# DLRM tower on one Trainium2 core: first indices in one small load spread by matmuls, first comparisons as tensor_scalar, another load order, and copies at a chunk's end split over two engines

## The reference

```python
e = jnp.stack([tbl_0[ids[:, 0]], ..., tbl_25[ids[:, 25]]], axis=1)      # (2048, 26, 128)
sd = jnp.einsum('bfd,bd->bf', e, dense)
ss = jnp.einsum('bfd,bgd->bfg', e, e)
z = jnp.concatenate([dense, sd, ss[:, iu, ju]], axis=1)                 # pairs above the diagonal
h = jnp.concatenate([z, dense], axis=1)
h = jnp.maximum(h @ W_top1 + b_top1, 0.0)                               # 607 -> 512
h = jnp.maximum(h @ W_top2 + b_top2, 0.0)                               # 512 -> 256
y = h @ W_top3
```

## Time and profile before

| | |
|---|---|
| time, 3 runs | median 418.59 us (418.02 to 419.38) |
| profiled execution | 415.0 us, its span 413.2 us |
| busy: PE, DVE, ACT, POOL | 344.1, 240.2, 191.2, 263.4 us |
| read from HBM | 34.90 MB |

### The profile page before, as it was taken

The page is one execution under the profiler, slowest core; times in us unless marked ns, Lnnn a source line. Parts: engine busy times, 40 slices in busy tenths (PEclk is TensorE's granted clock), DMA queues, the critical chain, the costliest instruction groups (busy, mean ns, idle before and its releaser), DMA issues.

```text
span 413.2 us, 12249 instructions
## 1 busy us (share of the span) xinstructions
PE 344.1 (83%) x5416; PEld 258.2 (62%) x5416; DVE 240.2 (58%) x454; ACT 191.2 (46%) x283; POOL 263.4 (64%) x279
## 2 busy tenths in 40 slices
PE   0816888569999998769999997879999996865797
PEld 0504445358878886357878885468778883554673
DVE  3827999538899860048799850068899720111421
ACT  2341103587712325756722326768413318794333
POOL 6777750377777777777777773777777755773000
PEclk9977998999999999869999999889999999996999
DMA  7998230133333322333333311424333211221000
GB/s 167 274 277 245 79 83 25 40 97 86 110 88 99 83 58 57 78 88 88 106 102 86 86 51 32 97 75 108 90 96 97 70 46 38 60 56 35 4 2 0
DMA packets 21332, 35.72 MB, mean 86 GB/s; under 512 B 8023, under 2 KB 10583, under 8 KB 21279
## 3 DMA queue, kind: packets, MB, share of 16 engines
q0 software_dynamic: 8704, 17.84, 17.0%
q1 hardware_dynamic: 12574, 17.09, 15.4%
HBM read 34.90 MB, written 0.01 MB: 84 GB/s over the span
## 4 chain that ended last, share of the span: by engine, by line
PE 64%; DVE 10%; DMA 8%; ACT 7%; issue 5%; POOL 5%; SPq 0%; POOLq 0%; ACTq 0%; DVEq 0%
PE late_bank L406 10%; PE late_bank L473 10%; PE gram_bank L440 10%; PE late_bank L407 9%; DVE one_hot L730 7%; PE turn_bank L424 6%; DMA table_ids<-in_ids_by_table_dram 6%; POOL rows L385 5%; PE turn_bank L406 4%; PE turn_bank L407 4%; ACT turned L617 3%; PE spare_bank L507 2%; PE late_bank L518 2%; PE gram_bank L507 2%; DVE table_lo L798 2%
## 5 line engine op out<-in xcount | busy, mean ns | idle before, releaser
L385 POOL DMA_INDIRECT rows<-in_tbl_dram,index x272 | 262.5, 965 | 113.0 <-issue 79.0
L730 DVE TENSOR_TENSOR one_hot<-table_ids,row_number 125x512 fp32r<-125x512 int32 x288 | 178.2, 681 | 39.9 <-PE turn_bank L407 15.3
L406 PE MATMUL late_bank<-one_hot,table_hi 125*128 125x512 f32 x192 | 85.9, 447 | 26.0 <-DVE one_hot L730 14.6
L617 ACT COPY turned<-turn_bank 128x512 f32<-128x512 f32 (+1 forms) x80 | 76.6, 1051 | 28.5 <-PE turn_bank L424 25.9
L407 PE MATMUL late_bank<-one_hot,table_lo 125*128 125x512 f32 x192 | 78.2, 407 | 0.0
L424 PE MATMUL turn_bank<-ident,rows 128*128 128x128 f32 x288 | 46.9, 293 | 24.1 <-ACT turned L617 17.6
L440 PE MATMUL gram_bank<-turned 128*27 128x26 f32 x4096 | 55.1, 194 | 12.7 <-issue 11.7
L406 PEld LDWEIGHTS late_bank<-one_hot,table_hi 125*128 125x128 f32 x192 | 37.9, 197 | 43.8 <-DVE table_lo L798 15.5
L440 PEld LDWEIGHTS gram_bank<-turned 128*27 128x27 f32 x4096 | 45.7, 107 | 28.8 <-issue 25.0
L284 DVE COPY gram<-gram_bank 124x208 f32<-124x208 f32 x32 | 12.0, 374 | 88.1 <-PE gram_bank L440 84.0
L424 PEld LDWEIGHTS turn_bank<-ident,rows 128*128 128x128 f32 x288 | 34.7, 149 | 37.4 <-issue 28.7
(11 more groups left out here) (64 smaller groups left out, 288.8 us busy)
## 6 DMA issues: line engine op xcount, KB each, us to landing
table_ids<-in_ids_by_table_dram SPq DMA_DIRECT2D x36, 256.0 KB, 3.3
rows<-in_tbl_dram,index POOLq DMA_INDIRECT x272
turned<-in_tbl_dram SPq DMA_DIRECT2D x6, 448.0 KB, 12.2
looked_up<-in_tbl_dram SPq DMA_DIRECT2D x3, 448.0 KB, 7.6
rows<-in_r_dense_features_dram SPq DMA_DIRECT2D x16, 64.0 KB, 2.4
gram<-in_W_top_dram SPq DMA_DIRECT2D x1, 702.0 KB
gram<-in_W_top_dram SPq DMA_DIRECT2D x2, 256.0 KB
looked_up<-in_W_top_dram SPq DMA_DIRECT2D x1, 512.0 KB
```

What stands on the lines that cost most here:

```text
L385: pool.indirect_dma_start(out=rows[:, row % RING_ROWS, :], out_offset=None, in_=tables[f], in_offset=bass.IndirectOffsetOnAxis(ap=index[:, ...
L406: pe.matmul(bank, table_hi[:, s, k, :], hot, start=k == 0, stop=False)
L617: nc.scalar.copy(to[:, f0:f1], of).then_inc(rows_copied, 1)
L730: nc.vector.tensor_tensor(one_hot[:, n % HOT_SLOTS, :], table_ids[0:RK, (c * LOOKUPS + s) % ID_SLOTS, :], row_number[0:RK, k:k + 1].broadc ...
```

## The change

1. **Indices of chunk 0.** The 9 broadcast loads of 256 KB are replaced by one load of the 26 index rows (26x512, 52 KB) into a slot of `table_ids`. VectorE casts them to float32; a TensorE matmul a table with a column of the identity, broadcast, as its weights writes that table's indices to 125 partitions of PSUM (`spread_ids`); ScalarE copies them to one of two slots at the end of `looked_up` (`copy_ids`). Later chunks load their indices as before.
2. **Comparisons of chunk 0** read this float32 copy and become `tensor_scalar` with a row number per partition in SBUF as the scalar. Those of later chunks stay `tensor_tensor` with the row numbers in PSUM.
3. **Order.** The index array for the gathers comes in three pieces (tile 0, tiles 1 to 3, the rest behind the weights) in place of two. The raw weights move to `gram` and one slot of `looked_up`. ScalarE rounds the tables between its other copies instead of all first, and splits the weights before the last two `copy_found`. Two memsets of PSUM fall away.
4. **Copies at a chunk's end and at the start.** Of tile 0, VectorE now does `place_found` and the row groups 1 and 3, ScalarE the groups 0, 2 and 4. `rows_copied` becomes two semaphores by bank. For tiles 1 to 3 nothing moves.

```diff
-            sp.dma_start(index[:, 0:1, :], index_tiles[:, 0:1, :]).then_inc(index_loaded[0], DMA)
-            load_ids(0, 0)
+            load_index(0)
+            sp.dma_start(id_rows, ids_t[:, 0:CHUNK]).then_inc(id_rows_loaded, DMA)
             load_table(0)
             load_dense(0, 0)
-            sp.dma_start(index[:, 1:, :], index_tiles[:, 1:, :]).then_inc(index_loaded[1], DMA)
-            load_table(1)
-            load_ids(0, 1)
-            for s in range(2, LOOKUPS):
+            load_index(1)
+            for s in range(1, LOOKUPS):
                 load_table(s)
-            load_dense(0, 1)
-            load_ids(0, ID_SLOTS)
+                if s == 4:
+                    load_dense(0, 1)
             for to, of in weight_loads:
                 sp.dma_start(to, of).then_inc(weights_loaded, DMA)
+            load_index(2)
...
+            def spread_ids(s):
+                if s == 0:
+                    pe.wait_ge(ident_made, 2)
+                    pe.wait_ge(id_values_made, 1)
+                if s >= ID_BANKS:
+                    pe.wait_ge(ids_copied, s - ID_BANKS + 1)
+                f = LOOKED_UP[s]
+                pe.matmul(id_bank(s), ident[0:26, f:f + 1].broadcast_to([26, RK]), id_values,
+                          start=True, stop=True).then_inc(ids_spread, 1)
+            for s in range(ID_BANKS):
+                spread_ids(s)
             for s in range(LOOKUPS):
                 pe.wait_ge(lo_made, s + 1)
                 look_up(0, range(s * K_ROWS, (s + 1) * K_ROWS))
+                if s + ID_BANKS < LOOKUPS:
+                    spread_ids(s + ID_BANKS)
...
+            round_table(0)
+            copy_ids(0)
+            round_table(1)
+            copy_ids(1)
+            round_table(2)
+            round_table(3)
+            for s in range(2, LOOKUPS):
+                copy_ids(s)
+                if s - 2 == LOOKUPS - 3:
+                    act.wait_ge(w1_merged, 1)
+                copy_found(0, range((s - 2) * K_ROWS, (s - 1) * K_ROWS))
+                if s + 2 < LOOKUPS:
+                    round_table(s + 2)
...
-                    nc.vector.tensor_tensor(one_hot[:, n % HOT_SLOTS, :], table_ids[0:RK, (c * LOOKUPS + s) % ID_SLOTS, :],
-                                            row_number[0:RK, k:k + 1].broadcast_to([RK, CHUNK]), ALU.is_equal).then_inc(one_hot_made, 1)
+                    hot = one_hot[:, n % HOT_SLOTS, :]
+                    if c == 0:
+                        last = nc.vector.tensor_scalar(hot, id_slot(s), row_number_sb[:, k:k + 1], None, ALU.is_equal)
+                    else:
+                        last = nc.vector.tensor_tensor(hot, table_ids[0:RK, (c * LOOKUPS + s) % ID_SLOTS, :],
+                                                       row_number[0:RK, k:k + 1].broadcast_to([RK, CHUNK]), ALU.is_equal)
...
                 if more:
-                    copy_rows(c + 1, 0, range(0, 2))
-                    place_found(c + 1, 0)
+                    copy_rows(act, c + 1, 0, (0,))
                 for n in range(N2):
                     relu2(c, n)
                 if more:
-                    copy_rows(c + 1, 0, range(2, TURNS))
+                    copy_rows(act, c + 1, 0, (2, 4))
                 copy_output(c)
...
                     split_h1(c, n)
+                if more:
+                    place_found(dve, c + 1, 0)
+                    copy_rows(dve, c + 1, 0, (1, 3))
```

More of the change, by code:

```diff
@@ L185, in dlrm_tower @@
         pairs = turned[:, (TILES - 1) % 2].rearrange("p i f -> p (i f)")[:, 0:GROUP * PAIRS].rearrange("p (q f) -> p q f", q=GROUP)
+        raw = [room[0:RK, n * K_ROWS * D:(n + 1) * K_ROWS * D]
+               for room in (looked_up[:, 0:LOOKUPS - 2].rearrange("p s b -> p (s b)"), turned[:].rearrange("p a i f -> p (a i f)"))
+               for n in range(room.shape[1] // (K_ROWS * D))][0:LOOKUPS]
         late_room = gram[:].rearrange("p a f -> p (a f)")
@@ L217, in dlrm_tower @@
         w2_lo_made = sem("w2_lo_made")
[L218 removed]
+        index_loaded = [sem(f"index_loaded{i}") for i in range(len(FIRST_TILES))]
+        id_rows_loaded = sem("id_rows_loaded")
+        id_values_made = sem("id_values_made")
+        ids_spread = sem("ids_spread")
+        ids_copied = sem("ids_copied")
         dense_loaded = [sem(f"dense_loaded{i}") for i in range(RING_TILES)]
@@ L693, in _, with round_table @@
             act.sem_inc(stored, DMA)
-            for s in range(LOOKUPS):
+            def round_table(s):
                 act.wait_ge(table_loaded[s], DMA)
```

161 lines of the change are left out of this document (90 added, 71 removed).

## The result

The changed kernel takes 395.67 us (median of 4 runs, 395.58 to 396.11) beside 418.99 us before (4 runs, 418.02 to 420.06): a ratio of 0.9445, 95% interval 0.9419 to 0.9471. That is 23.3 us faster, or 19.3 us by the profiled executions (415.0 to 395.68; spans 413.2 to 393.9). The forecast was 404.4 with a range of 398 to 413: a gain of up to 20.6 us, which the 23.3 between the medians exceed and the 19.3 between the profiled executions would not. Medians leave out disturbed runs.

The account below looks back on a forecast made before the run. The prediction took TensorE as the main bound, with VectorE pacing the start and GpSimd's gathers the last chunk. Its terms, 19.0 - 5.0 - 5 + 5.2 = 14.2 us, off the 418.6 us median gave 404.4, range 398 to 413.

Parts of the forecast that it names:

- 19.0: Start: the most TensorE can be ahead at chunk 0's last gathers before GpSimd limits it, 19.0 us instead of 25.1.
- the holding: Start: VectorE work delays gathers, 5.0 us by `table_lo`, splits and `place_found`, and 5 us by the new comparisons.
- the ends: Chunk ends: splitting the copies lets group 4 be turned 2.6 us sooner at each of two ends, 5.2 us; the third counts nothing.
- the level: Total time: the 14.2 us gain is taken off the 418.6 us median, 3.6 above the profiled execution's 415.0.
- x = 5: Start: what the 72 new comparisons cost by stretching gathers, taken as 5 us.
- the one moment of a gather: Start: a comparison delays a gather only by catching one moment of it, for half its own length, 3.3 us in all.
- a hold for 65% of every comparison: Start: comparisons hold gathers for as large a part of their length as seven `table_lo` operations did, 16 us.
- the end hardly depends on it: Start: whether a comparison takes 0.34 us or stays at 0.60 was said to matter little to the final time.
- a rival at 403.3: Start: comparisons stay at 0.60 us and hold no gathers, gain 15.3 us, time 403.3; chance 0.13.
- first product at 59.5: End of the start: TensorE's first product comes at 59.5 instead of 84.65, up to 25.1 us ahead.
- GpSimd still waiting before tile 12: Last chunk: GpSimd still waits for tile 12's rows; if not, it bounds everything and the third-end argument changes.
- The rival "Slower": Start: each comparison waits for the gather in flight, one per 1.247 us, time about 445; chance 0.06.

Follow-up runs that it names:

- the doubled kernel: The changed kernel with each of chunk 0's comparisons made twice, once into an unused buffer: 423.18 us, ratio 1.0136 to the kernel before.
- `mix`: The changed kernel with the last four tables' comparisons of chunk 0 as `tensor_tensor`, the first five as changed: 396.41 us, ratio 0.9492 to the kernel before.

## Why the prediction was right or wrong

**The mechanism was right in the main.** The start was shortened until gathers bounded it, TensorE waits for them in the last tile of chunk 0 (at 87.95, 92.99 and 97.91, though not in the tile before it, as expected too), stretched gathers take some of it back, both kinds of term add up, and a comparison takes 0.40 us from start to start instead of 0.60. The Trainium skill, "VectorE: DVE Perf Modes", The perf-mode tier table, has the two forms at two elements and one a cycle. The trace (0.40 and 0.60 us) agrees with the direction; by halving the elements at an unchanged fixed part the forecast had 0.34, so the fixed part is larger here. Its sum was 19.0 - 5.0 - 5 + 5.2 = 14.2 us of span; measured were 13.6 to the end of chunk 0, 8.8 over the next two chunks and -3.2 behind tile 12, 19.3 unrounded.

**Three terms were mis-sized, all in the same direction:** the holding by 4.6 us (13.6 where 19.0 - 10 = 9.0 was forecast), the ends by 3.6, and the level by 4.0. The tail took 3.2 back, and the median of the kernel before came out 0.4 higher than the one that the forecast started from. That is the 8.7 us between 404.4 and 395.67. The result lies 2.3 us below the range, so by this sum any one of the three, had it been right, would have kept it inside.

**The failed step in the mechanism: what a chunk's end is worth.** The prediction put "2 x 2.6 = 5.2 us". Measured: 8.8, in the changed kernel and in that with the ends alone. The 2.6 was how much sooner group 4 could be turned, and that held: it is turned 4.31 us behind group 0 (147.33 to 151.64) where it was 7.07 (160.97 to 168.04), 2.8 us sooner. It left out what follows the wait. Layer 3's 3.25 us stood in the rows and was taken as a fixed price, though the same four matmuls take 1.88 when TensorE has stood idle for only 0.97 us ahead of them. That is 1.4 us more, and 2.8 + 1.4 are the 4.1 to 4.2 us by which an end got shorter (10.59 to 6.46). Another 0.3 of the 4.4 is spread over the chunk and not traced.

**Mis-sized: the holding.** The prediction took 5.0 for `table_lo`, splits and `place_found`, and x = 5 for the comparisons, 10 in all. Measured in the start: 11.0 of excess against 5.5 before, so 5.5 or so, of which the comparisons have about 2. 19.0 - 5.5 = 13.5 is within 0.3 of the 13.6 and 13.8 us at the end of chunk 0: the limit that GpSimd sets there was right. Of the two laws behind x, the one moment of a gather that a comparison can hold (3.3 us by the prediction's working) came near the 2 us of the changed kernel, and a hold for 65% of every comparison (16) did not. But neither foresees gathers of 7.17 us, and twice the comparisons cost 27.6 us more instead of 2. So x = 5 was between two laws of which one fits this kernel and none fits both. That the holding stayed small here may be luck: the doubled kernel shows that a gather can last through 16 comparisons in a row, and not what brings that about.

**Wrong: "the end hardly depends on it".** With slower comparisons the kernel takes 400.21 instead of 395.67 (each beside its own runs of the kernel before, so uncertain by some 3 us). The prediction had this as a rival at 403.3, 1.1 us better than its forecast, so it held the faster comparison to be worth nothing or less; it was worth 4.5 us, or 5.4 by the start of the last gather, which is the firmer figure. Its first product at 59.5 was 65.95 in truth: a table goes every 4.97 us, where 3.8 and most of a spreading matmul of 0.81 were counted, and the row groups take 1.08 us each on VectorE, not 0.68. That price stood in the earlier trace rows, where ScalarE made two such copies in 2.09 us; the prediction took that of a contiguous piece. That cost nothing, since 13.8 of the 18.7 us of lead were all that could be used.

**Wrong: "GpSimd still waiting before tile 12".** The prediction named this as the sign that would change its last step. With ends worth 4.4 and holding worth 5.5, GpSimd's waits at 253.84 and 343.37 are used up, and it runs without a stop from the first gather to the last. The right sum for this case was GpSimd's ledger, 28.9 - 7.3, though its second term was known only afterwards.

**Not foreseen: the tail.** Behind the last gather the changed kernel needs 39.6 us and the first profile of before 37.2, with the same 504 matmuls; the granted clock was 0.92 and 0.94. But before's own second profile needed 38.9 there at 0.90, so only some 0.7 of the 2.4 us are left to be blamed on the change.

**Mis-sized: the level.** The prediction took its gain off the median because the profiled execution of before was 3.6 us under it. That assumes the same distance in the changed kernel, and there is none: its profiled execution took 395.68, its median is 395.67. So the gain between medians was 23.3, 4.0 more than between profiles; 418.6 - 19.3 would have been 399.3, inside the range. The second profile of before (418.41, near its median) gives the sum that belongs to the medians: 15.2 us to the first chunk's end (162.48 to 147.33), 9.1 over the next two (181.8 to 172.7) and -1.6 behind, 22.7. What was lost in a usual execution of before, 1.5 us in the start and 1.7 behind the last gather, is TensorE's time, and the start's part is hidden once GpSimd sets the pace. That a kernel paced by GpSimd is shielded from such spread was not tested: the first four runs of the changed kernel spread over 0.5 us and the four of before over 2.0, but `mix`, in which GpSimd waits for nothing either, spread over 2.6.

The rival "Slower", by VectorE waiting for gathers, found nothing for it: in the start VectorE's comparisons keep their 0.40 us even beside a gather of 7.17, so it is GpSimd that waits.

## What to carry to other kernels

A wait of TensorE can cost more than its length, because matmuls behind it may run at the lower clock: before counting a removed wait, compare the duration of the matmuls behind it with the same shape elsewhere. When the bound moves to an engine that makes gathers, sum that engine's own ledger (its true waits, less what stretches its work), and check whether the other terms have used up its slack. When VectorE gets a faster form whose inputs are both in SBUF, read the durations of the gathers beside it: here most of them grew by 0.2 to 0.3 us, and a few, with twice as many comparisons, by 6.2. And before a gain from two profiles is taken off a median, look where the profiled execution stands among the runs of either kernel.

## What the runs showed of the hardware that was not expected

- **A gather can take 7.17 us** beside 16 `tensor_scalar` of 0.48 us in a row, ending 0.12 us after the last of them, and 1.28 beside another such row of the same kernel (19.09 to 25.43). Which it is, no run explains. VectorE's comparisons kept their 0.40 us from start to start in both.
- **Four matmuls of 512 columns with one column of weights** took 1.88 us after 0.97 us of idle time (granted clock 1.00) and 3.25 to 3.56 after 3.5 us (0.56 over the first of them), in every chunk's end read whose four records are complete.
- **A copy from PSUM whose destination elements lie 108 apart** (a row group, 128x512) took 1.08 us on VectorE in the start and 1.05 on ScalarE (two in 2.09), against 0.59 for ScalarE's copy of 512 elements to adjacent places in the earlier trace rows.
- **Two chips ran both kernels 60% slower.** There TensorE's instructions came apart, with nothing that they waited for. Its timeline in the second run of the changed kernel:

```profile
84.40 0.20 PE L500 MATMUL gram_bank<-turned 128*27 128x26 f32 x1 [1.22 <-issue]
86.50 0.37 PE L481 MATMUL turn_bank<-ident,rows 128*128 128x128 f32 x1 [1.90 <-issue]
87.90 0.37 PE L481 MATMUL turn_bank<-ident,rows 128*128 128x128 f32 x1 [1.03 <-issue]
90.70 0.37 PE L481 MATMUL turn_bank<-ident,rows 128*128 128x128 f32 x1 [2.43 <-issue]
```

Recorded transposes stand 1.40 and 2.80 us apart, where eight take 1.06 us elsewhere; between 66 and 84 us the granted clock was 0.56 and TensorE busy for 3.37 us, while gathers went on every 1.25 us undisturbed. The page counts 5434 matmuls, as many as for this kernel on an ordinary chip. A transpose took 0.37 us there, which does not space them so far, so the cause is open. The ratio of the two kernels was nearly kept, 0.953 against 0.945.
